# An attention and mixture-of-experts kernel: norms and routing cut in pieces around each tile's reciprocal, routing one group later

## What is computed

```
x = x + attention(layernorm(x), ctx)          # 4 x 1024 tokens of width 256, 16 heads of 64, 77 keys, gamma/beta norm inside
x = x + ffn(layernorm(x))                     # both in float32

attention(q, c):  p = softmax((q Wq + bq) (c Wk + bk)^T);  r = q + (p (c Wv + bv)) Wo + bo
                  gamma * (r - mean) * rsqrt(var + 1e-3) + beta
ffn(n):           w, e = top_k(softmax(n Wg), 4)          # 32 experts
                  for each expert: its first 2048 (token, expert) pairs, swiglu(W1, W3, W2) * w, added up
                  plus a shared swiglu(Ws1, Ws3, Ws2) over all tokens
```

## Time and profile before

| | us |
|---|---|
| median of 3 runs | 891.05 (888.31 to 892.07) |
| the profiled execution | 892.84 |
| its span in the profile | 891.1 |
| PE busy | 776.5 (87%) |
| DVE busy | 524.6 (59%) |
| ACT busy | 448.2 (50%) |
| POOL busy | 377.2 (42%) |

### The profile page before, as it was taken

One profiled execution on the slowest core, in us unless ns is written; L12 is line 12 of the kernel. 1 busy time (PEld: TensorE's weight loads), 2 busy tenths in 40 slices (PEclk: granted clock), 3 DMA queues, 4 the chain that ended last, 5 costly groups with the idle time before them and its releaser, 6 DMA issues.

```text
span 891.1 us, 17145 instructions
## 1 busy us (share of the span) xinstructions
PE 776.5 (87%) x3710; PEld 586.3 (66%) x3711; DVE 524.6 (59%) x1496; ACT 448.2 (50%) x1834; POOL 377.2 (42%) x352
## 2 busy tenths in 40 slices
PE   7777999999898989899779849998999998999870
PEld 5564677777676767576635528786877887886440
DVE  1763235858686776869575315554555554553578
ACT  3454877676766676666513003554555554554000
POOL 1001233257473828383871603554555654565000
PEclk9979999999999999999877978999999999999995
DMA  6335322335353535597375975666665554563996
GB/s 238 99 128 159 110 83 83 110 126 181 113 196 104 188 106 187 159 356 212 120 255 195 332 243 190 219 194 194 183 226 166 183 179 146 181 183 116 352 361 221
DMA packets 132865, 164.29 MB, mean 184 GB/s; under 512 B 11253, under 2 KB 120771, under 8 KB 132803
## 3 DMA queue, kind: packets, MB, share of 16 engines
q1 hardware_dynamic: 118979, 121.66, 43.5%
q0 software_dynamic: 13824, 41.96, 13.0%
HBM read 84.77 MB, written 78.81 MB: 184 GB/s over the span
## 4 chain that ended last, share of the span: by engine, by line
PE 56%; DVE 20%; DMA 8%; issue 6%; ACT 5%; SPq 4%; DVEq 1%; ACTq 0%; POOLq 0%
PE psum L1475 14%; PE psum L1250 10%; PE psum L1330 9%; PE psum L1372 8%; PE psum L1487 7%; PE psum L1414 4%; DVE big L1228 3%; DMA xblk<-expert_lists 3%; ACT sm L781 2%; DMA big<-in_x 2%; DVE ln1g L939 2%; PE psum L1425 2%; DVE x L976 2%; PE psum L1393 2%; SPq L536 2%
## 5 line engine op out<-in xcount | busy, mean ns | idle before, releaser
L672 POOL DMA_INDIRECT y_d<-sm,yrow x160 | 154.9, 968 | 154.0 <-issue 89.6
L1475 PE MATMUL psum<-big,xbT 128*128 x640 | 169.6, 388 | 0.7 <-DVE xbT L1200 0.4
L781 ACT ACTIVATE sm<-psum,nmax 128x77 f32<-128x77 f32 x512 | 157.5, 366 | 16.2 <-DVE nmax L1089 16.2
L1372 PE MATMUL psum<-big,pT 128*128 (+1 forms) x640 | 150.4, 392 | 2.0 <-DVE res L1104 2.0
L658 POOL DMA_INDIRECT expert_lists<-rows,slot x128 | 126.3, 987 | 57.4 <-issue 38.6
L1330 PE MATMUL psum<-big,xnT 128*128 (+2 forms) x384 | 138.9, 510 | 3.3 <-ACT sm L781 2.7
L639 POOL TENSOR_TENSOR sm<-sm,sinv 128x1232 f32<-128x1232 f32 x32 | 72.1, 2253 | 158.9 <-DVE sinv L1113 158.6
L1372 PEld LDWEIGHTS psum<-big,pT 128*128 128x128 f32 x640 | 124.2, 198 | 19.0 <-DVE res L1104 2.2
L781 ACT ACTIVATION_READ_ACCUMULATOR sm<-psum,nmax 128x1 f32 x512 | 127.4, 249 | 0.0
L1475 PEld LDWEIGHTS psum<-big,xbT 128*128 128x128 f32 x640 | 111.4, 194 | 12.3 <-issue 3.3
L1330 PEld LDWEIGHTS psum<-big,xnT 128*128 128x128 f32 x384 | 70.1, 190 | 59.7 <-issue 50.9
(11 more groups left out here) (180 smaller groups left out, 1038.0 us busy)
## 6 DMA issues: line engine op xcount, KB each, us to landing
xblk<-expert_lists SPq DMA_DIRECT2D x160, 160.0 KB, 2.3
y_d<-zero SPq DMA_DIRECT2D x32, 512.0 KB, 4.0
big<-y_d SPq DMA_DIRECT2D x32, 512.0 KB, 8.6
big<-in_L_ffn_W SPq DMA_DIRECT2D x16, 320.0 KB
expert_lists<-filler SPq DMA_DIRECT2D x32, 160.0 KB, 2.8
xin<-in_x SPq DMA_DIRECT2D x36, 128.0 KB, 2.1
big<-in_x SPq DMA_DIRECT2D x8, 512.0 KB, 3.5
xres<-in_x SPq DMA_DIRECT2D x8, 512.0 KB, 5.2
```

What stands on the lines that cost most here:

```text
L672: pool.indirect_dma_start(out=y_d, out_offset=bass.IndirectOffsetOnAxis(ap=yrow[:, q:q + 1], axis=0), in_=eo[:, q, :], in_offset=None).the ...
L781: last = nc.scalar.activation(sm[:, t % 2, h * SK:(h + 1) * SK], head_scores(h, h + 1), ACT.Exp, bias=nmax[:, t % 2, h:h + 1], accum_out=s ...
L1372: last = mm(o_ps[:, 0:D], pT[:, to % 2, c, :], VO[:, bass.ds(batch(jo, po), 1), c, :], start=c == 0, stop=c == CK - 1)
L1475: last = mm(bank(2 + q % 2)[:, 0:2 * H], xbT[:, q % 2, k, :], ew[:, bass.ds(e, 1), k * 2 * H:(k + 1) * 2 * H], start=k == 0, stop=k == KC - 1)
```

## The change

Nothing of what is computed changes. In each group:

- DVE: `second_norm` becomes aggregation and scaling (behind the reciprocal of t=1) and `second_scale`, the reciprocal square root (ahead of the reciprocal of t=2). `third_norm` becomes `residual` (x2, ahead of the reciprocal of t=2), `third_norm` (statistics, behind it) and `third_scale` (ahead of the reciprocal of t=3). `choose` becomes `choose` (t=1, ahead of the reciprocal), `mark` (t=1, behind it) and `label` (t=3, behind it). `place` moves to t=0 of the group after, ahead of the reciprocal.
- ACT and PE: `rows` moves from t=2 to t=3, transposes of rows, xn2T, gate and logits from t=3 to t=0 of the next group; prefix counts from t=1 to t=2, pos from t=1 to t=3.
- POOL: the scatters go from 8 + 8 in t=2 and t=3 for the group two back to 4 + 6 + 6 in t=0, 1 and 2 for the group three back.
- Four groups instead of two are written out ahead of the loop on DVE and POOL; the drain is cut at other steps.

```
@@ POOL
-                if t >= 2 and live(*ago(j, p, 2)):
-                    jh, ph = ago(j, p, 2)
-                    if t == 2:
+                if t < 3 and live(*ago(j, p, 3)):
+                    jh, ph = ago(j, p, 3)
+                    if t == 0:
                         wait(pool, "rows_ready", (num(jh, ph) + 1) * TG)
...
-                    for tt in ((0, 1) if t == 2 else (2, 3)):
-                        for k in range(TOPK):
+                    for i in range(*((0, 4), (4, 10), (10, 16))[t]):
+                        tt, k = i // TOPK, i % TOPK
@@ ACT
-                if t == 1 and live(j2, p2):          # pos
+                if t == 3 and live(j2, p2):
...
-                if t == 3 and live(jh, ph):
-                    move_xn2T(jh, ph, 0)
+                if t == 0 and live(j2, p2):
+                    move_xn2T(j2, p2, 0)
...
-                if t == 0 and live(j2, p2):          # exp of the shifted logits
+                if t == 1 and live(j2, p2):
...
-                if t == 3 and live(jh, ph):          # logits
-                    wait(act, "logits_psum", num(jh, ph) + 1)
+                if t == 0 and live(j2, p2):
+                    wait(act, "logits_psum", num(j2, p2) + 1)
...
-                if t == 2 and live(jh, ph):          # rows; inside: wait(act, lists_ready[ph], jh * (16 * TG * TOPK))
+                if t == 3 and live(jh, ph):
...
-            drain(step, 2, TG)
+            drain(step, 2, TG + 1)
             shared_silu(1, 0)
-            drain(step, TG + 1, 2 * TG - 1)
+            drain(step, TG + 2, 2 * TG - 1)
@@ DVE, step
+                g1, g2, g3 = (ago(j, p, d) for d in (1, 2, 3))
-                if t == 0 and live(*ago(j, p, 2)):
-                    shift_logits(*ago(j, p, 2))
+                if t == 1 and live(*g2):
+                    shift_logits(*g2)
                 ... nmax ...
+                if t == 0 and live(*g3):
+                    place(*g3)
-                if t == 0 and live(*ago(j, p, 2)):
-                    choose(*ago(j, p, 2))
-                if t == 1 and live(*ago(j, p, 2)):
-                    place(*ago(j, p, 2))
-                if t == 2 and live(*ago(j, p, 1)):
-                    third_norm(*ago(j, p, 1))
+                if t == 1 and live(*g2):
+                    choose(*g2)
+                if t == 2 and live(*g1):
+                    second_scale(*g1)
+                    residual(*g1)
+                if t == 3 and live(*g1):
+                    third_scale(*g1)
                 ... res of tile n-2 ...
-                if t == 1 and live(*ago(j, p, 1)):
-                    second_norm(*ago(j, p, 1))
                 ... reciprocal ...
+                if t == 1 and live(*g2):
+                    mark(*g2)
+                if t == 1 and live(*g1):
+                    second_norm(*g1)
+                if t == 2 and live(*g1):
+                    third_norm(*g1)
+                if t == 3 and live(*g2):
+                    label(*g2)
...
-            drain(step, 3, TG)
+            drain(step, 3, TG + 1)
             shared_gate(1, 0)
             add_shared(0)
-            drain(step, TG + 1, 2 * TG - 1)
+            drain(step, TG + 2, 2 * TG)
@@ PE
-                if t == 1 and live(j2, p2):          # prefix counts
+                if t == 2 and live(j2, p2):
...
-                if t == 3 and live(jh, ph):          # also the second half and the gate product
-                    wait(pe, "rows_ready", num(jh, ph) * TG + 2)
-                    transpose_rows(jh, ph, 0)
+                if t == 0 and live(j2, p2):
+                    wait(pe, "rows_ready", num(j2, p2) * TG + 2)
+                    transpose_rows(j2, p2, 0)
```

More of the change, by code:

```diff
@@ L310, in wrap, with phase1 @@
             return n % size
-        def phase1(eng, step):
-            for g in range(2):
+        def phase1(eng, step, first=1):
+            for g in range(2 * first):
                 for t in range(TG):
-                    step(0, g, t)
-            with eng.Fori(1, NG // 2) as j:
+                    step(g // 2, g % 2, t)
+            with eng.Fori(first, NG // 2) as j:
                 for p in range(2):
@@ L631, in _ @@
             pool.wait_ge(s["ld_bc"], 32)
[L632 removed]
+            slots_due = counter(pool, "slot_ready", 2, 1)
             def step(j, p, t):
@@ L655, in step @@
                         slots_due(num(jh, ph) + 1)
-                    for tt in ((0, 1) if t == 2 else (2, 3)):
-                        for k in range(TOPK):
-                            pool.indirect_dma_start(
-                                out=lists, out_offset=bass.IndirectOffsetOnAxis(ap=slot[:, ph, tt, k:k + 1], axis=0),
-                                in_=rows[:, ph, tt, :], in_offset=None).then_inc(lists_ready[ph], 16)
-            phase1(pool, step)
-            drain(step, 0, 2 * TG - 1)
+                    for i in range(*((0, 4), (4, 10), (10, 16))[t]):
+                        tt, k = i // TOPK, i % TOPK
+                        pool.indirect_dma_start(
+                            out=lists, out_offset=bass.IndirectOffsetOnAxis(ap=slot[:, ph, tt, k:k + 1], axis=0),
+                            in_=rows[:, ph, tt, :], in_offset=None).then_inc(lists_ready[ph], 16)
+            phase1(pool, step, 2)
+            drain(step, 0, 2 * TG + 2)
             pool.wait_ge(s["zeroed"], 16 * NT)
@@ L964, in second_norm, with second_scale, residual @@
                                                    ALU.subtract, ALU.mult).then_inc(s["scaled_ready"], 1)
+            def second_scale(jh, ph):
+                g = num(jh, ph)
+                wait(dve, "mv2_ready", (g + 1) * TG)
                 rsqrt(dve, "ln2_step", g * RSQRT_OPS, mv2[:, :, 1], EPS_ATT, nw2)
-            def third_norm(jh, ph):
+            def residual(jh, ph):
                 g = num(jh, ph)
@@ L977, in third_norm @@
                                                    xres[:, ph, t, :], ALU.mult, ALU.add).then_inc(s["x2_ready"], 1)
+            def third_norm(jh, ph):
+                g = num(jh, ph)
                 for t in range(TG):
@@ L983, in third_norm, with third_scale @@
                     nc.vector.bn_aggr(mv3[:, t, :], st3[:, t, :]).then_inc(s["mv3_ready"], 1)
+            def third_scale(jh, ph):
+                g = num(jh, ph)
                 wait(dve, "rows_ready", g * TG)
@@ L1019, in choose, with mark @@
                     nc.vector.max_index(topi[:, t, :], top[:, t, :], prob[:, t, :]).then_inc(s["topi_ready"], 1)
+            def mark(jh, ph):
+                g = num(jh, ph)
                 wait(dve, "topi_ready", (g + 1) * TG)
@@ L1031, in choose, with label @@
                 wait(dve, "mask_ready", g + 1)
+                wait(dve, "prefix_psum", g)
                 nc.vector.tensor_reduce(gsum[:, :], mask[:, :, :].rearrange("p t e -> p e t"), AX, ALU.add
                                         ).then_inc(s["gsum_ready"], 1)
+                wait(dve, "gsum_ready", g + 1)
+                nc.vector.tensor_tensor(before_sum[:, 1 - ph, :], before_sum[:, ph, :], gsum[:, :], ALU.add
+                                        ).then_inc(s["earlier_ready"], 1)
+            def label(jh, ph):
+                g = num(jh, ph)
                 wait(dve, "pair_ready", g)
@@ L1039, in choose @@
                                         .to_broadcast([P, TG * TOPK, E]), ALU.mult).then_inc(s["pairs_e_ready"], 1)
-                wait(dve, "prefix_psum", g)
-                wait(dve, "gsum_ready", g + 1)
-                nc.vector.tensor_tensor(before_sum[:, 1 - ph, :], before_sum[:, ph, :], gsum[:, :], ALU.add
-                                        ).then_inc(s["earlier_ready"], 1)
                 wait(dve, "pairs_e_ready", g + 1)
@@ L1374, in step @@
                     last.then_inc(s["out_psum"], 1)
-                if t == 3 and live(jh, ph):
-                    wait(pe, "xn2T_sbuf", num(jh, ph) * 2 + 1)
-                    wait(pe, "rows_ready", num(jh, ph) * TG + 4)
-                    transpose_rows(jh, ph, 1)
+                if t == 0 and live(j2, p2):
+                    wait(pe, "xn2T_sbuf", num(j2, p2) * 2 + 1)
+                    wait(pe, "rows_ready", num(j2, p2) * TG + 4)
+                    transpose_rows(j2, p2, 1)
                 if live(jm, pm):
@@ L1388, in step @@
                             last.then_inc(s["pt_psum"], 1)
-                if t == 3 and live(jh, ph):
-                    wait(pe, "xn2T_sbuf", num(jh, ph) * 2 + 2)
+                if t == 0 and live(j2, p2):
+                    wait(pe, "xn2T_sbuf", num(j2, p2) * 2 + 2)
                     for tt in range(TG):
@@ L1431, in _ @@
             s_up(0, 1)
-            drain(step, 2, TG - 1)
+            drain(step, 2, TG)
             s_up(1, 0)
             s_down(0)
-            drain(step, TG, 2 * TG - 1)
+            drain(step, TG + 1, 2 * TG - 1)
             pe.wait_ge(s["earlier_ready"], NG)
```

21 lines of the change are left out of this document (10 added, 11 removed).

## The result

| | before | changed |
|---|---|---|
| median of 20 runs, us | 891.73 | 895.35 |
| profiled execution, us | 892.84 | 893.59 |
| its span | 891.1 | 891.8 |
| last output product of phase 1 starts | 444.93 | 444.52 |
| fillers start | 490.09 | 492.98 |

The changed kernel is slower by 0.55%: ratio 1.0055 [1.0038, 1.0072]. The prediction was 884.4 us, faster; the sign was wrong, the time lies inside the range, 0.6 us from its upper end.

What follows compares the result with a forecast made beforehand. PE was taken to bound the kernel, idle in phase 1 mainly waiting for `rows`, about 4 us lost per group. Phase 1 -16.6 and drain +10.0 gave -6.6: 891.05 to 884.4 us, range 874 to 896.

Steps and rivals of the forecast that it cites:

- PE's waits before: Phase 1 of the kernel before: seven waits for `rows`, 14.4 us in total, and two single ones in the drain.
- Groups 1 to 3: Phase 1: step of group 1 takes 39.2 us, groups 2 and 3 take 43.1 each.
- 0.45 us of wait at the prefix counts: PE in t=2: mask ready at S2+4.65, wanted at S2+4.15, so 0.45 us of new wait.
- Who goes first behind the reciprocal: DVE and POOL, t=1: POOL's product goes first and holds up DVE's pieces for all its 2.25 us.
- rival 1: Behind t=1's reciprocal, one-hot precedes POOL's product: DVE loses 0.8, not 2.25; groups 4 to 7 43.6; 876 us, chance 0.26.
- The list wait: End of group steps: ACT's `rows` waits for scatters in groups 3 to 7, leaving PE 1.7 us idle.
- groups 4 to 7: 45.0 each: Phase 1 loop: each of these four group steps takes 14.8+9.77+10.6+9.77 = 45.0 us, 180.0 together.
- rival 2: PE's clock: new idle time slows output products, about 1.2 us in each of 4 groups; 889.2 us, chance 0.16.
- rival 3: Last scatter lands after 4.0 us beside expert weights, `rows` 1.2 later, slow products: 11.2 on top, 895.6 us, chance 0.20.
- Phase 1 in all: From first group with a norm to the last group's end: 417.3 against 433.97, -16.6 us.
- The drain: Behind phase 1's groups: +4.7 to the last output product, +3.35 for third_scale, +1.9 for label, +10.0 us in all.
- the forecast's 22.0: Drain, to the last output product's end: idle 5.9, transposes, products and gate, 22.0 us against 17.3 before.

Runs made afterwards that it cites:

- f2: Changed kernel with ACT's loop starting at group 4 instead of group 2, so it turns once (at group 6): 884.49 us, 0.990 of the kernel before.
- f3: Changed kernel with ACT's phase 1 written out, the last group's third_scale before the shared gates, fill positions before label and place: 879.25 us, ratio 0.984.
- f1: Changed kernel run again unaltered, on one chip with its variants: 895.78 us, 1.0035 of the kernel before.
- f4: Changed kernel with the last group's expert weight loads all issued in the drain instead: 902.64 us, 1.010 of the kernel before.
- h1: Changed kernel with ACT's loop begun one tile later, so it turns once, between tiles 0 and 1 of group 4: 883.33 us, ratio 0.989.
- h3: f3 with the last xn2T_d load behind the fillers and group 7's weight loads two by two behind tiles 2 and 3: 880.37 us, ratio 0.986.
- h4: f2 with the mark put back ahead of the reciprocal of tile 1: 892.74 us, 1.001 of the kernel before.

## Why the prediction was wrong

- **PE's waits before.** The list that the forecast starts from left out four waits for `sm`, 3.3 us in all; in the changed kernel one of 0.9 is left. The slips in its sums are small: 12.6 + 2.3 + 0.1 + 0.35 + 1.6 is 16.95 and not 16.8, and gsum ends at 304.02 and not 303.95.
- **Groups 1 to 3**, 39.2, 43.1, 43.1: measured 39.1, 42.7, 42.7. Right but for the 0.45 us of wait at the prefix counts, which did not come.
- **Who goes first behind the reciprocal.** Taken: the product, 2.25 us. Measured: cast and one-hot start at 312.58 and 312.73 and the product behind them at 312.76, as rival 1 and as the Trainium skill's rule (SBUF — State Buffer, Who interferes with whom: whichever instruction issues first keeps the pair) would have it. The 0.17 against 0.33 us of the earlier trace rows came again as 0.15 against 0.33, and the register instruction between did not change it. The nmax of tile 2 then starts 5.3 us behind its scores (312.10 to 317.42) and not 7.05, which fits that undisturbed groups take 43.4 to 43.8 us and not 45.0: of the 1.3 us in group 5, 0.9 lie in tile 0, with the shorter wait for `rows`, and 0.4 at the prefix counts, where no wait appeared. Rival 1's 43.6 was right; its 42.2 for groups 2 and 3 was 0.5 too low.
- **The list wait.** Right in kind: ACT's `rows` waits for the scatters in all five places. Its size was 1.7 us on PE in the forecast and 0.35 to 0.84 in groups 4 to 6.
- **What failed: "groups 4 to 7: 45.0 each".** The sum set every group of the loop alike. Two things differ between them, and neither was in it: the turn of ACT's loop, and in group 7 the weight loads (next point). The turn: the diff was read step by step, but not where the step's boundary, and so the jump, would come to stand. Between 240.43 and 246.08 it is on the only path that PE waits for. It cost 8.0 us in group 4 (51.4 against 43.4 in f2) and 6.1 in group 6 (49.9 against 43.8 in f3); on the chip of f2 and f3 themselves, with f1 in place of the first trace, 6.9 and 4.8. Of the 8.0, 3.45 are idle time (3.85 against 0.40 in f2), 1.65 the slower gate (3.62 against 1.97) and 2.7 the slower scores (7.10 against 4.38). The amplification is rival 2's; its starting point was not.
- **Group 7.** Rival 3 had the cause, expert weights beside the scatters, but took 4.0 us from the earlier trace rows as the worst landing; it was 5.9 to 6.6, and in one group, not in four. Of the 48.15 us 3.95 are the wait, and the output product behind it takes 6.17 instead of 4.48; with the loads moved away (f4) the group is 4.8 us shorter.
- **Phase 1 in all.** Forecast -16.6, measured -4.4 (111.94 to 433.97, against 112.48 to 430.1). The gap of 12.2 is +6.4, -1.3, +4.9 and +3.2 in groups 4 to 7 and -1.0 in groups 1 to 3.
- **The drain.** Forecast +10.0, measured +6.8: 19.0 us from the end of tile 3 to the end of the last output product, against 17.3 (+1.7, not +4.7: the idle time was 4.7, not 5.9, and gate and last product took 6.3 together, where the forecast's 22.0 leaves 7.65 for them), and 43.9 against 38.8 from there to the fillers (+5.1, forecast 5.25).
- **The sum** of start (+0.5), phase 1 and drain is +2.9 at the fillers; the span is longer by only 0.7, so 2.2 us came back behind them in this execution; the cause stays open.
- **The range** held it, but for the wrong mechanism at its slow end: rival 3 was worth 3.2 us of its 11.2. That the measured 895.35 lies 0.3 us from rival 3's 895.6 is luck.

With one turn fewer (f2) or the turn hidden (h1) the order is what was hoped for: they are 1.0 and 1.1% faster than the kernel before. f3, which also has the two edits in the drain, is 1.6% faster, with h3 (1.4%, the intervals overlap) the fastest here.

## What to carry to other kernels

When code moves between steps of a loop, find each engine's jump back in the new order and ask who waits for the first instruction behind it; put the jump where that engine waits for another one anyway. Allow for idle time of PE costing about twice its length when matrix work follows at once (here 3.45 us more of it cost 8.0, and 1.5 more cost 3.3), since the clock that it loses is paid in the next products. It need not: the 2.30 us in front of 330.19 were followed by products at full clock. And price each group of a loop by what runs beside it there: the average of a landing time hides the group in which other loads share the DMA engines.

## What the hardware showed that I had not expected

- A turn of ACT's loop over two groups cost 3.0 to 3.8 us of idle time in the changed kernel and 0.9 to 1.0 in f2 and h4, with the same loop body on ACT; what makes the difference was not tried.
- PE fell from full clock to 0.50 behind 3.85 us without work, and to 0.58 in the stretch behind 1.91 us. In the kernel before it stayed at 1.00 behind 2.30 us (328 to 344 us).
- Scatters to the lists land in 5.9 to 6.7 us beside weight loads, with the DMA share at 0.93 to 1.11 (374 to 390 us, changed kernel), and in 2.5 to 2.9 with those loads moved away, with the share at 0.34 to 0.73 (f4, 374 to 382 us).
- Chips differ by more than this change: 893 and 914 us for the kernel before. On the slower one the three variants of the changed kernel were 1.3 to 2.4% behind it, with a standstill of 9.4 to 10.7 us in the drain that no run on the others has.
